# Condition products and the first chunk's rows of a two-layer sequence model, moved within one kernel

## The reference

```python
x = x + attn0(lstm0(x, cond, ...), ...)               # linear attention
x = x + ffn0(rnn(x, cond, ...), ...)                  # 16 experts, top 2
x = x + attn1(lstm1(x, cond, ...), ...)               # layer norm, softmax attention, 8 heads
x = x + ffn1(gru(video=cond, seq=x, ...), ...)        # 8 experts, top 4, one shared

def gru(video, seq, W_z, U_z, C_z, b_z, ...):         # gates z, r and the candidate h
    vz = video @ C_z + b_z; vr = video @ C_r + b_r; vh = video @ C + b
    xz = seq @ W_z; xr = seq @ W_r; xh = seq @ W
    # a step: z = sigmoid(xz_t + h @ U_z + vz), r likewise,
    #         hh = tanh(xh_t + (r * h) @ U + vh), h = (1 - z) * h + z * hh
```

## Time and profile before

| | |
|---|---|
| runs | 2739.54, 2740.47, 2743.89 us; median 2740.47 |
| profiled execution | 2751.23 us, span 2749.4 us |
| TensorE busy | 2434.8 us (89%) |
| VectorE busy | 1926.3 us (70%) |
| ScalarE busy | 1154.4 us (42%) |
| GpSimd busy | 398.2 us (14%) |
| mean granted clock of TensorE | 0.947 |

### The profile page before, as it was taken

One profiled execution on the slowest core, in us unless ns is written; L12 is line 12 of the kernel. 1 busy time (PEld: TensorE's weight loads), 2 busy tenths in 40 slices (PEclk: granted clock), 3 DMA queues, 4 the chain that ended last, 5 costly groups with the idle time before them and its releaser, 6 DMA issues. The chain is left out here.

```text
span 2749.4 us, 119339 instructions
## 1 busy us (share of the span) xinstructions
PE 2434.8 (89%) x50848; PEld 2038.0 (74%) x50848; DVE 1926.3 (70%) x7408; ACT 1154.4 (42%) x3690; POOL 398.2 (14%) x413
## 2 busy tenths in 40 slices
PE   1668999999999999987858868999999999999999
PEld 0455677777777777754536658999999999999998
DVE  4567777777777777788666656766766667766674
ACT  3124555555555555556336733333333333333333
POOL 0000000000000000000009701222222222222222
PEclk9778999999999999999769958999999999999999
DMA  5000000000000000010013230000000000000000
GB/s 170 1 2 3 5 5 5 5 6 5 5 5 5 6 5 5 3 45 27 4 43 105 74 97 22 9 9 9 9 9 9 9 9 9 9 9 9 5 5 6
DMA packets 52747, 53.66 MB, mean 20 GB/s; under 512 B 24934, under 2 KB 46840, under 8 KB 50042
## 3 DMA queue, kind: packets, MB, share of 16 engines
q1 hardware_dynamic: 46868, 26.81, 3.7%
q0 software_dynamic: 2000, 14.68, 1.5%
q10 hardware_dynamic: 3350, 4.54, 0.5%
HBM read 39.46 MB, written 6.55 MB: 17 GB/s over the span
## 5 line engine op out<-in xcount | busy, mean ns | idle before, releaser
L105 PE MATMUL p<-xn,m_h 128*128 128x128 f16 x6144 | 557.5, 219 | 0.0
L105 PE MATMUL p<-xn,m_l 128*128 128x128 f16 x3072 | 528.8, 219 | 0.0
L105 PEld LDWEIGHTS p<-xn,m_h 128*128 128x128 f16 x6144 | 479.9, 98 | 1.8
L576 PE MATMUL lg_b<-xn,lh 128*32 128x256 f16 x6144 | 298.4, 290 | 79.8 <-DVE lh L1016 77.9
L2052 POOL TENSOR_TENSOR xn<-qkv_w,xn 128x384 f16<-128x384 f32 x256 | 234.0, 914 | 904.3 <-ACT xn L2010 904.3
L992 DVE STREAM_TRANSPOSE gt<-lg_b 128x512 f32<-128x512 f32 x324 | 230.1, 710 | 189.7 <-PE lg_b L576 189.3
L814 ACT ACTIVATE gl<-gt 128x128 f32<-128x128 f32 x324 | 100.2, 309 | 603.8 <-DVE gt L992 603.1
L829 ACT ACTIVATE hm<-xy,b 128x512 f32<-128x512 f32 x512 | 347.4, 679 | 0.2
L105 PEld LDWEIGHTS p<-xn,m_l 128*128 128x128 f16 x3072 | 300.6, 98 | 0.7
L1936 PE MATMUL po<-m_h,xn 128*128 128x256 f16 x1536 | 292.6, 272 | 1.9 <-DVE xn L2091 1.9
L576 PEld LDWEIGHTS lg_b<-xn,lh 128*32 128x32 f16 x6144 | 158.8, 101 | 165.0 <-DVE lh L1016 130.1
(11 more groups left out here) (386 smaller groups left out, 6208.5 us busy)
## 6 DMA issues: line engine op xcount, KB each, us to landing
m_stage<-in_m_w POOLq DMA_DIRECT2D x12, 1024.0 KB, 5.2
hs<-in_m_w SPq DMA_DIRECT2D x14, 384.0 KB, 3.3
xs<-in_x POOLq DMA_DIRECT2D x1, 2048.0 KB, 8.5
x_dram<-x SPq DMA_DIRECT2D x16, 128.0 KB, 2.1
xs<-in_l_wv SPq DMA_DIRECT2D x1, 2048.0 KB
attention_dram<-att SPq DMA_DIRECT2D x16, 128.0 KB, 2.8
xn<-x_dram SPq DMA_DIRECT2D x16, 128.0 KB, 2.5
out_dram<-xn SPq DMA_DIRECT2D x16, 128.0 KB, 2.2
```

Source lines behind the costliest of these rows:

```text
L105: ins = pe.matmul(out, w[wp](k), x[xp](k), start=start, stop=last and k == KT - 1 and xp == 1, skip_group_check=True)
L576: last = pe.matmul(gate_block(ae, j, par), lh[:, part, ae, k, u, :], columns(w[name], k, j), start=False, stop=(part == 1 and k == KT - 1) ...
```

## The change

1. The condition products move into round 0 of the first stage. SyncE issues their nine loads at the start of that stage's main block; the weights go to `hm32`, the bias row to `s_ab`. TensorE makes group m after `lstm_step` of slot 6 + m, into the bank `z`; VectorE splits them at slot 13. The `ones2` memset moves along.
2. In the last batch of the second attention VectorE divides head 0's first 128 queries by themselves at iteration 58, once `values(56)` is done (`rinv0`, `att0`); `values(57)` waits for it. SyncE then stores these rows, loads the x2 rows and the four pieces of down weights, waits for the store and for the stores of earlier batches, loads the eight rows of chunk 0, waits until all are there, and only then waits for the last batch's division and stores it. That store writes head 0's rows a second time.
3. TensorE turns the rows after its last `values`, into the bank `pj`; VectorE adds and splits them after the last division. The first block of the second pipeline keeps the memsets and the half projection.
4. The attention stage no longer ends with a wait for its stores; that wait heads SyncE's work in the scan's block. All eight row loads go through SyncE's queue (four went through ScalarE's), and the four pieces too.

```diff
 # pipeline_one, SyncE, TensorE, GpSimd and VectorE
+            for g, n in enumerate("zrh"):
+                r = slice(g * D, (g + 1) * D)
+                sp.dma_start(s_c[:, :, r], t["g_c" + n].rearrange(k2, p=P)).then_inc(vt_in, 16)
+                sp.dma_start(s_gb[0:1, r], t["g_b" + n].rearrange(row, a=1)).then_inc(vt_in, 16)
+            sp.dma_start(s_cz[:, :, :], t["cond"].rearrange(k2, p=P)).then_inc(vt_in, 16)
+            sp.dma_start(late.own[:, :, :], t["k_own"]).then_inc(vt_in, 16)
+            sp.dma_start(late.iota[:, :, :].rearrange("p e j -> p (e j)"), t["k_iota4"]).then_inc(vt_in, 16)
...
+            def condition(m):
+
+                if m == 0:
+                    pe.wait_ge(vt_in, 144)
+                    pe.wait_ge(vt_one, 2)
+                o = z[:, m * B:(m + 1) * B]
+                pe.matmul(o, s_gb[0:1, m * P:(m + 1) * P], s_one[0:1, :], start=(m == 0), stop=False,
+                          skip_group_check=True)
+                for k in range(KT):
+                    last = pe.matmul(o, s_c[:, k, m * P:(m + 1) * P], s_cz[:, k, :], start=False, stop=(k == KT - 1),
+                                     skip_group_check=True)
+                last.then_inc(vt_pe, 1)
...
                 lstm_step(i, slot)
+                if i == 0 and 6 <= slot < 12:
+                    condition(slot - 6)
+                if (i, slot) == (1, 0):
+                    pe.wait_ge(vt_read, 2)
...
+            pool.memset(s_one[0:1, :], 1.0).then_inc(vt_one, 1)
+            pool.memset(late.ones2[:, :], 1.0).then_inc(vt_one, 1)
...
+                if (i, slot) == (0, 13):
+                    vz = z[:, 0:6 * B].rearrange("p (m b) -> p m b", b=B)
+                    dve.wait_ge(vt_pe, 6)
+                    dve.tensor_scalar(late.vt_h[:, :, :], vz, S, None, ALU.mult).then_inc(vt_read, 1)
+                    dve.wait_ge(vt_read, 1)
+                    dve.scalar_tensor_tensor(out=late.vt_l[:, :, :], in0=vz, scalar=S, in1=late.vt_h[:, :, :],
+                                             op0=ALU.mult, op1=ALU.subtract).then_inc(vt_read, 1)
 # attention_two, SyncE
-            for dst, src in late_loads:
-                sp.dma_start(dst, src).then_inc(g_loaded, 16)
             for b in range(B):
+                if b == B - 1:
+
+                    sp.wait_ge(early_att, 1)
+                    sp.dma_start(rows[b, :, 0:1, 0, :], att0[:, :].unsqueeze(1)).then_inc(rows_out, 16)
+                    sp.dma_start(rooms["x2r"], x2d[:, :, LAG * CW:(LAG + 1) * CW]).then_inc(rows_in, 16)
+                    for n in range(4):
+                        sp.dma_start(down_piece(hs1, n), t["m_w3"][:, GM * n:GM * (n + 1), :]).then_inc(m3_staged[n], 16)
+                    sp.wait_ge(rows_out, 16)
+                    sp.wait_ge(att_sent, 16 * TT * b)
+                    for bb in range(B):
+                        o = bb * T * D
+                        sp.dma_start(rooms["attr"][bb * C:(bb + 1) * C, :],
+                                     attd[o:o + C * D].rearrange("(t d) -> t d", d=D)).then_inc(rows_in, 16)
+                    sp.wait_ge(rows_in, 16 * (B + 1))
                 sp.wait_ge(att_done, b + 1)
                 for s_ in range(TT):
                     sp.dma_start(rows[b, :, :, s_, :], att[:, :, s_, :]).then_inc(att_sent, 16)
-            sp.wait_ge(att_sent, 16 * TT * B)
-            sp.wait_ge(g_loaded, 16 * len(late_loads))
 # TensorE
                 pe.wait_ge(pt_lo, g + 1)
+                if g == GH - NH + 1:
+                    pe.wait_ge(early_att, 1)
...
-                if 0 <= g - VPS < 6:
...
+            pe.wait_ge(rows_in, 16 * (B + 1))
+            pe.wait_ge(pj_lo, 3 * B)
+            for k in range(KT):
+                last = pe.matmul(xps[:, k * P:(k + 1) * P], rooms["attr"][:, k * P:(k + 1) * P], ident[:, :],
+                                 is_transpose=True, start=(k == 0), stop=True, skip_group_check=True)
+            last.then_inc(x_tr, 1)
 # VectorE
-                if g == VPS + 7:
...
+                if g == GH - NH + 2:
+
+                    dve.wait_ge(pv_pe, GH - NH + 1)
+                    dve.reciprocal(rinv0[:, :], sums[:, (B - 1) % 2, 0, 0:1]).then_inc(early, 1)
+                    dve.wait_ge(early, 1)
+                    dve.tensor_scalar(att0[:, :], po[:, 0, 0, :], rinv0[:, 0:1], None, ALU.mult).then_inc(early_att, 1)
+
+            x0, gx_h, gx_l = hs1[:, :, 0:CW], rooms["gx_h"], rooms["gx_l"]
+            dve.wait_ge(x_tr, 1)
+            dve.tensor_tensor(x0.rearrange("p k (t b) -> p k t b", b=B),
+                              xps.rearrange("p (k b t) -> p k t b", k=KT, b=B),
+                              rooms["x2r"].rearrange("p k (t b) -> p k t b", b=B), ALU.add).then_inc(x_out, 1)
+            dve.wait_ge(x_out, 1)
+            dve.tensor_copy(gx_h, x0).then_inc(x_out, 1)
+            dve.wait_ge(x_out, 2)
+            dve.tensor_tensor(gx_l, x0, gx_h, ALU.subtract).then_inc(x_out, 1)
 # pipeline_two: the first block keeps GpSimd's memsets and project_half(pe, 0); then, in the scan's block
             def _(sp):
+                sp.wait_ge(att_sent, 16 * TT * B)
             load_rows(sp, 1, rows_in)
```

More of the change, by code:

```diff
@@ L416, in pipeline_one @@
             sem(n) for n in ("om_hi", "om_split", "x2_done", "x2_split", "x2_sent"))
+        vt_in, vt_one, vt_pe, vt_read = (sem("vt_" + n) for n in ("in", "one", "pe", "read"))
         pre_a, pre_q, pre_g, v_sum, prep_hi, prep_lo, prep_set, row_in, rows_out = (
@@ L1318, with attention_two @@
 PJ_SCALE = (float(DK) ** -0.5 / S, 1.0 / S, 1.0 / S)
-def attention_two(nc, t, hs1, attd, m12_h, m12_l, late, qkv):
+def attention_two(nc, t, hs1, attd, x2d, m12_h, m12_l, late, qkv, att_sent, m3_staged):
     with ExitStack() as ctx:
@@ L1651, with pipeline_two @@
 Z3_AT = {k: n for n, k in enumerate((i, slot) for i in range(NCH + 2) for slot in z3_uses(i))}
-def pipeline_two(nc, t, arena, attd, x2d, m12_h, m12_l, late, qkv, out):
+def pipeline_two(nc, t, arena, attd, x2d, m12_h, m12_l, late, qkv, att_sent, m3_staged, out):
     with ExitStack() as ctx:
@@ L1722, in pipeline_two @@
         x3_done, x3_split, out_done = (sem(n) for n in ("x3_done", "x3_split", "out_done"))
-        m3_staged = [sem(f"m3_staged{j}") for j in range(4)]
         m3_hi, m3_lo = sem("m3_hi_done"), sem("m3_lo_done")
@@ L2256, in build_kernel @@
         m12_h, m12_l = sb("m12_h", [P, 2, KT, NT, P]), sb("m12_l", [P, 2, KT, NT, P])
-        attention_two(nc, t, hs1, attd, m12_h, m12_l, late, qkv)
-        pipeline_two(nc, t, hs1, attd, x2d, m12_h, m12_l, late, qkv, out)
+        att_sent = ctx.enter_context(nc.semaphore("att_sent"))
+        m3_staged = [ctx.enter_context(nc.semaphore(f"m3_staged{j}")) for j in range(4)]
+        attention_two(nc, t, hs1, attd, x2d, m12_h, m12_l, late, qkv, att_sent, m3_staged)
+        pipeline_two(nc, t, hs1, attd, x2d, m12_h, m12_l, late, qkv, att_sent, m3_staged, out)
 def _layout(d):
```

103 lines of the change are left out of this document (30 added, 73 removed).

## The result

| | before | after |
|---|---|---|
| median, 20 runs each | 2741.55 us (2739.0 to 2759.29) | 2736.86 us (2723.61 to 2740.83) |
| ratio | | 0.9967, 95% interval 0.9954 to 0.9979 |
| profiled execution, span | 2751.23 us, 2749.4 us | 2728.55 us, 2726.5 us |

The forecast was 2724.3 us with a range of 2719 to 2732: the sign was right, the median lies 4.9 us above the range. The runs stand in two groups. Of the 20 after, 9 lie between 2723.6 and 2733.1 and 11 between 2736.7 and 2740.8; of the 20 before, 17 lie between 2739.0 and 2743.9 and 3 between 2753 and 2759.

A forecast was written before the change was run, and what follows sets the result against it. It took the seam before the scan (14.37 us with nothing else running) and TensorE in the last heads as the bound. -7.3 - 9.6 + 0.7 = -16.2 us gave 2735.0, less 10.8 of gap 2724.3 us; range 2719 to 2732.

The forecast's parts named there:

- Part 1: Last heads of the second attention: condition products removed, heads then run at ScalarE's 1.72 us each, -7.3 us.
- the rival in which the clock comes back: TensorE returns to 2.4 GHz in the last heads and over the seam, 2.0 us more gain, 2722.3 us; chance 0.10.
- Part 2: Seam between second attention and scan: stores not waited for, rows turned beside the division; 4.8 us for 14.37, -9.6 us.
- VectorE's three operations: In the seam after the last division: add, cast and subtract on the rows, 1.27 us.
- the middle boundary: Block boundary in the seam between VectorE's operations and the half projection, taken as 0.5 us.
- the half projection: In the seam: half of the first chunk's gate products with the boundary behind it, 3.04 us up to the scan.
- the turn of the rows: On TensorE behind the last value products: hides beside the 0.69 us division if the rows are there.
- Part 3: SyncE's early store and row loads during the last heads: landed by 1592.4, hidden before TensorE finishes head 63, 0 us.
- 1.5 us of spare: Margin between the row loads landing at 1592.4 and TensorE finishing head 63 at 1593.9.
- Part 4: Round 0 of the first stage: condition products fit TensorE's idle time in five plain steps, overrun step 9, +0.7 us.
- The gap: Profiled execution 10.8 us above the three-run median 2740.47; carried over whole, taking the forecast from 2735.0 to 2724.3 us.

The follow-up runs named there:

- skip9: Changed kernel with the condition products moved off slot 9, to slots 6, 7, 8, 10, 11 and 12 of round 0: 2733.44 us, ratio 0.9959 to the kernel before.
- pad: Changed kernel with condition products late in the first stage, plus 24 small VectorE copies heading the second attention: 2730.44 us, ratio 0.9933 to the kernel before.
- b1: The kernel before, run again unchanged for a second trace: 2751.84 us, ratio 1.0014, profiled span 2735.4 us.

## Why the prediction failed

**Part 1, the heads: mechanism right, 2 us too small.** The forecast let them run at ScalarE's 1.72 us a head; they ran at 1.50. The rows that gave 1.72 were read as free of projections, and they are not. TensorE makes the next batch's projections among them (busy 7.81 of 8 us from 1556 to 1564, at a granted clock of 1.00), and ScalarE itself converts two of their results. This is ScalarE in the kernel before:

```profile
1558.14 0.59 ACT L1556 ACTIVATE v_h<-pj 128x512 f16<-128x512 f32 x1
...
1561.15 0.60 ACT L1548 ACTIVATE pt_h<-pt 128x512 f16<-128x512 f32 x1
...
1562.65 0.60 ACT L1548 ACTIVATE pt_h<-pt 128x512 f16<-128x512 f32 x1
1563.14 0.59 ACT L1556 ACTIVATE q_h<-pj 128x512 f16<-128x512 f32 x1
```

The head between the two conversions takes 1.50 us (1561.15 to 1562.65), which is the pace of the last heads after the change, where no projection is left. In the last heads of the changed kernel the granted clock was 1.00, and a turn took 0.64 us in place of 1.09. The last batch is shorter by 9.3 where 7.3 stood. So the rival in which the clock comes back was half true: it came back for the heads, not for the seam.

**Part 2, the seam: right but for 0.7 us.** 14.37 us became 5.42, -8.95 for -9.6. Its terms: VectorE's three operations 1.22 (1.27 forecast), the middle boundary 0.31 (0.5), the half projection 3.02 (3.04). What was missed is the turn of the rows: it was to hide beside the division and ended 0.8 us after it, because it waited 0.92 us for them (part 3).

**Part 3, the row loads: 0 forecast, 0.9 us of wait measured.** SyncE was through in 6.8 us, not 7.6 (1576.67 to 1583.46), and the first load was issued 0.1 us behind the last piece, so the store, which landed 1.8 us after its issue, held up nothing. But the eight loads landed later than their forecast 1.8 us. This is the row loads' line in the changed kernel (issue in ns; us from issue to landing, both min/median/max):

```profile
L1456 SPq DMA_DIRECT2D xn<-attention_dram x8: 363/420/421, 1579.9 to 1583.0; - x8
...
DMA to landing us min/median/max: 3.2/3.8/4.6
```

I had used the median over 124 loads spread over the whole scan for eight that stand in a burst, with the pieces ahead of them (the DMA share is 1.00 in 1580 to 1582). Whether the pieces delay them was not tested; no run has the rows ahead of the pieces. The heads also ended sooner, so the 1.5 us of spare became a wait of 0.92. The Trainium skill, DMA: Bandwidth & Descriptors, Specifications, says that transfers under 512 bytes miss the line rate; this store's 1.8 us is near the low end of the 1.5 to 5.2 that the prediction feared, and the trace shows no lateness that the kernel feels.

**Part 4, round 0: the step that failed in the sum.** I took +0.7, because idle time before each step held the product, and +0.7 is what step 9 lost (4.37 us, 3.68 in skip9). The prediction also read both of its rows as at the lower clock; the second, 0.99 us long, straddles the rise at 94.7, and in the changed kernel that idle time is gone. The step that failed is that idle time covers the products, so that what does not overrun costs nothing. Measured is +3.7, of which 1.5 in round 0 and 1.9 in rounds 1 and 2, where no product was added. In the trace the products fill idle time while the granted clock stays at 0.50 with TensorE busy 78% of the time (18.64 of 24 us), and the steps are longer at that level. That the products hold the clock down is the reading that fits the loss behind them; it was not separated from the loads. The prediction had the observation in hand: in the heads it saw thin f32 products with the clock at 0.50 and wrote that they count for little, and used it only for what their removal might give, not for what their arrival would cost. The Trainium skill, TensorE: Matmul & The Clock Gate, What's actually happening, states that the throttle is released by how busy the engine has been; by busy share alone, round 0 disagrees as the earlier trace rows did.

**The scan: a term that was not there.** +1.4 us, by which and how many steps are long. The prediction put the scan at no change without a term; the kernel before had no row for one, and it could have had either sign, as pad shows.

**The gap: the step that failed in the base.** "The stretches I change hold no part that I can tie to this gap, so I carry the difference over whole." The prediction carried 10.8 us of gap between the profiled execution and the median. Between that execution and b1, 14.0 us apart, 9.7 were the long form of the tail, 74.5 in place of 64.9 us, and 3.1 the attention's batches, both by the granted clock. Taking the gap off made 2724.3 the time of a run with the short tail, where 9 of 20 runs were (2723.6 to 2733.1), and gave the long tail no place in the range, though the trace in hand was a run with it. With the sum corrected (-12.7) and 11 of 20 runs in the upper group, the median lies near the upper group, and the range should have reached up to that group.

In short: forecast -16.2, by its own steps -12.7 in the traces; ratio -9.0 in the first comparison, with -12.7 at the edge of its interval (-12.6 to -5.8); median -4.7. Of the 12.6 us by which the median missed 2724.3, the sum's terms are 3.5; the other 9 are about the length of the gap that was taken off. That the two kernels' medians stand in different forms of the tail would explain them, but only profiled runs have a trace, so for the medians this is argued. The first set of runs was also an unlucky one for the median: in the three later ones it is 14.0, 9.0 and 5.8 us below that of the kernel before.

## What to carry over

Idle time of an engine is a cover only if what is put there does not slow what stands around it: on TensorE, look also at the granted clock that small f32 products leave behind them, not at their own length alone. When a profiled execution lies far above the median of the runs, find out which stretch is the long one before any difference is carried over; it may be a form that the changed kernel draws too. A pace is to be read from rows that hold what the changed stretch will hold, and nothing more. And a few instructions added in front of a long loop can move its time by 1 to 3 us, so a sum of parts is not good to better than that.

## What I had not expected

- One kernel has a stretch that takes 63 to 79 us with the same instructions, at a mean granted clock of 0.80 and 0.55. That is over half of a per cent of the whole time.
- 24 copies that cost nothing where they stand shortened the scan behind them by 1.7 to 2.4 us.
- Six groups of products of at most 1.6 us each, in one round of 57 us, cost 3.7 us, most of it over three rounds, and taking them off slot 9 won nothing.
